# Attention: four steps' weights summed on GpSimd before each group of denominators, and the router's weight product moved into earlier stages

## The reference

```python
x = x + _L0_gnn_ref(_layernorm(x, axis=-1), adj, ...)
x = x + _L0_ffn_ref(_layernorm(x, axis=-1)[None], ...)[0]

# in the second layer
scores = jnp.einsum('bhqd,bhkd->bhqk', q, k) / jnp.sqrt(jnp.float32(HD))
scores = jnp.where(causal, scores, -jnp.inf)
attn = jax.nn.softmax(scores, axis=-1)
y = jnp.einsum('bhqk,bhkd->bhqd', attn, v)
return y.transpose(0, 2, 1, 3).reshape(b, s, d) @ w_o
...
logits = xf.astype(jnp.float32) @ w_router.astype(jnp.float32)
```

## Time and profile before

| | |
|---|---|
| median of three executions | 2271.41 us (2270.23 to 2273.5) |
| the profiled execution | 2268.96 us |
| its span, first to last instruction | 2267.2 us |
| busy in it: PE, DVE, ACT, POOL | 2055.1, 1553.6, 1078.9, 584.4 us |
| mean granted TensorE clock | 0.952 |
| first values product of the attention to its last | 1009.0 to 1683.1 us |

### The profile page before, as it was taken

One profiled execution on the slowest core, in us unless ns is written; L12 is line 12 of the kernel. 1 busy time (PEld: TensorE's weight loads), 2 busy tenths in 40 slices (PEclk: granted clock), 3 DMA queues, 4 the chain that ended last, 5 costly groups with the idle time before them and its releaser, 6 DMA issues. The chain is left out here.

```text
span 2267.2 us, 42225 instructions
## 1 busy us (share of the span) xinstructions
PE 2055.1 (91%) x17716; PEld 1213.2 (54%) x17716; DVE 1553.6 (69%) x2563; ACT 1078.9 (48%) x1059; POOL 584.4 (26%) x447
## 2 busy tenths in 40 slices
PE   6899999999996899989999999999991599999997
PEld 3554444444442344544444444444430599999997
DVE  6679999999984666757777778768347544444442
ACT  4868988989890333213444444444430233323331
POOL 2610000000002012333454555555340222222211
PEclk8989999999998999969999999999995699999999
DMA  6521212212115013343103121010203444444431
GB/s 227 182 79 51 72 52 74 69 52 78 49 52 199 25 47 102 130 112 72 36 16 87 31 64 49 20 38 10 80 24 130 158 121 121 121 121 121 116 66 24
DMA packets 90905, 185.87 MB, mean 82 GB/s; under 512 B 14332, under 2 KB 23548, under 8 KB 86332
## 3 DMA queue, kind: packets, MB, share of 16 engines
q1 hardware_dynamic: 81756, 162.20, 21.8%
q0 software_dynamic: 8960, 20.98, 5.0%
HBM read 138.47 MB, written 40.23 MB: 79 GB/s over the span
## 5 line engine op out<-in xcount | busy, mean ns | idle before, releaser
L1473 DVE TENSOR_REDUCE t_rm<-t_m 128x1 f32<-128x512 f32 (+3 forms) x640 | 372.8, 605 | 150.2 <-PE t_m L1622 96.8
L1407 ACT ACTIVATE t_E<-t_s 128x1024 f32<-128x1024 f32 (+3 forms) x320 | 277.4, 895 | 412.3 <-PE t_s L1639 223.8
L1369 POOL TENSOR_TENSOR t_total<-t_E 128x1024 f32<-128x1024 f32 (+2 forms) x151 | 292.4, 1947 | 221.4 <-PE t_d L1666 215.6
L573 ACT ACTIVATE m_step<-m_ub,gat_bias 128x2048 bf16<-128x2048 f32 x128 | 250.0, 1989 | 11.1 <-DMA m_ub<-scratch_uac 5.7
L715 PE MATMUL m_bd<-m_mask,m_S 128*32 128x512 bf16 x3072 | 230.4, 379 | 10.9 <-DVE m_mask L663 10.9
L715 PE MATMUL m_bd<-gat_adjT,m_S 128*32 128x512 bf16 x2496 | 201.4, 379 | 4.8 <-PE m_dn L715 4.8
L715 PE MATMUL m_bd<-m_mask,m_neg 128*32 128x512 bf16 x2496 | 189.0, 379 | 0.0
L1996 POOL DMA_INDIRECT out<-e_ye,e_token x40 | 80.7, 2018 | 339.1 <-DVE e_ye L2099 334.4
L2160 PE MATMUL e_h<-e_xTh,e_w1h 128*128 128x320 f32 x512 | 159.1, 311 | 1.4 <-DVE e_xTl L2080 1.4
L2160 PE MATMUL e_h<-e_xTh,e_w1l 128*128 128x320 f32 x512 | 158.8, 310 | 0.0
L2160 PE MATMUL e_h<-e_xTl,e_w1h 128*128 128x320 f32 x512 | 158.8, 310 | 0.0
(11 more groups left out here) (359 smaller groups left out, 4085.7 us busy)
## 6 DMA issues: line engine op xcount, KB each, us to landing
a_adj<-in_adj SPq DMA_DIRECT2D x16, 1024.0 KB, 4.9
m_ub<-scratch_uac SPq DMA_DIRECT2D x16, 1024.0 KB, 5.0
e_w1r<-in_L_ffn_w SPq DMA_DIRECT2D x8, 2048.0 KB, 8.2
e_w2r<-in_L_ffn_w SPq DMA_DIRECT2D x8, 2048.0 KB, 8.8
tq_Q<-scratch_parts SPq DMA_DIRECT2D x36, 256.0 KB, 4.6
gat_scale<-scratch_uac SPq DMA_DIRECT2D x32, 256.0 KB
scratch_parts<-o_hi SPq DMA_DIRECT2D x32, 256.0 KB, 2.2
scratch_parts<-o_lo SPq DMA_DIRECT2D x32, 256.0 KB, 2.7
```

The lines of the kernel that those rows point to most:

```text
L573: act.activation(step(n), ub[h % 2][:, :].rearrange("p (t q) -> p t q", t=T), ACT.Relu, bias=bias[:, j, h:h + 1], scale=BIG).then_inc(step ...
L1369: pool.tensor_tensor(total[:, two, off:BANK], E[a % 3][:, two, off:BANK], E[(a + 1) % 3][:, two, off:BANK], ALU.add).then_inc(summed[z], 1)
L1407: act.activation(E[n % 3][:, two, off:BANK], ps_s[:, two, off:BANK], ACT.Exp, scale=SCALE).then_inc(exp_done[z], 1)
L1473: dve.tensor_reduce(rm[:, h, t, ch:ch + 1], ps_m[i % 2][:, 0:w], AX, ALU.max).then_inc(entry_read, 1)
```

## The change

Two parts. In the attention, `total` now holds the sum over four steps: GpSimd adds in three of four steps (E + E, then total + E twice, `add_step`), and one group of denominators, always 512 columns wide, follows for the four. It stands in TensorE's order in step 4k+5, ahead of `values(4k+5)`, where the group of steps 4k to 4k+3 is taken; there are 40 groups. GpSimd waits for `den_done` of the group before only at the first of its three additions. `BY_VECTOR` covers the same part of the last quad, from step 144, in the new grouping; rows are added to the residual one step later in GpSimd's order. In the first stages, the clearing of WG and the scaling of G move to `stage_sequence` (the latter ahead of the product of tile 14), columns 0 and 1 of WG follow the last transposes of that stage, column 2 stands ahead of the first transposes of `stage_factors`, column 3 between its second and third; ScalarE copies the first two at the end of `stage_sequence` and the others where it copied all four.

```diff
+WG_EARLY = 2
+def router_columns(pe, keep, bank, k):
+    for b in range(KD):
+        mm = pe.matmul(bank[:, EXPERTS * k:EXPERTS * (k + 1)], keep["woT"][:, b, k * P:(k + 1) * P],
+                       keep["G"][:, b, :], start=(b == 0), stop=(b == KD - 1))
+    return mm
 # stage_sequence, GpSimd
+                pool.memset(keep["WG"][:, :, :], 0.0).then_inc(g_ready, 1)
                 for t in range(T - 1):
+                    if t == T - 2:
+                        pool.wait_ge(late_in, 16 * (KD + 2))
+                        pool.tensor_tensor(keep["G"][:, :, :], keep["G"][:, :, :], ..., ALU.mult).then_inc(g_ready, 1)
 # stage_sequence, ScalarE, behind store(T - 1)
+                act.wait_ge(wg_early, WG_EARLY)
+                act.activation(keep["WG"][:, 0:WG_EARLY, 0:EXPERTS], ...)
 # stage_sequence, TensorE, behind turn(T - 1)
+                pe.wait_ge(g_ready, 2)
+                for k in range(WG_EARLY):
+                    router_columns(pe, keep, ps_t[0], k).then_inc(wg_early, 1)
 # stage_factors, TensorE
                     if n == 0:
+                        router_columns(pe, keep, late, WG_EARLY).then_inc(wg_full, 1)
                         pe.wait_ge(u_ready, 1)
                     if n == 2:
+                        for k in range(WG_EARLY + 1, KD):
+                            router_columns(pe, keep, late, k).then_inc(wg_full, 1)
                         pe.wait_ge(exp_done, 1)
...
-                pe.wait_ge(g_ready, KD + 3)
-                for k in range(KD):
-                    for b in range(KD):
-                        mm = pe.matmul(p1[...], woT[:, b, k * P:(k + 1) * P], G[:, b, :], ...)
-                mm.then_inc(wg_full, 1)
 # stage_attention
+    FOUR = 4
+    SUMS = []
+    for n in range(QUADS * NS):
+        first_pair = 2 if STEPS[n % NS - n % FOUR + 1][2] else 1
+        SUMS.append((SUMS[-1] if n else 0) + (first_pair, 0, 1, 1)[n % FOUR])
-    BY_VECTOR = [k for k in range(QUADS * NS // 2) if 2 * k >= (QUADS - 1) * NS + HALF + 1]
+    BY_VECTOR = range((QUADS - 1) * NS + HALF + FOUR, QUADS * NS)
+        def add_step(eng, n, z):
+            off, two = STEPS[n % NS][2], slice(2 * z, 2 * z + 2)
+            eng.wait_ge(exp_done[z], n + 1)
+            if n % FOUR == 1:
+                if n >= FOUR:
+                    eng.wait_ge(den_done, n // FOUR)
+                if off:
+                    eng.tensor_copy(total[:, two, 0:off], E[(n - 1) % 3][:, two, 0:off]).then_inc(summed[z], 1)
+                before = E[(n - 1) % 3]
+            else:
+                eng.wait_ge(summed[z], SUMS[n - 1])
+                before = total
+            eng.tensor_tensor(total[:, two, off:BANK], before[:, two, off:BANK],
+                              E[n % 3][:, two, off:BANK], ALU.add).then_inc(summed[z], 1)
 # GpSimd
-                for k in range(QUADS * NS // 2):
...
+                for n in range(QUADS * NS):
+                    if n % FOUR:
+                        for z in range(1 if n in BY_VECTOR else 2):
+                            add_step(pool, n, z)
+                    if n >= (QUADS - 1) * NS:
+                        while added < EARLY and STEP_OF[added] < n % NS - 2:
                             add_row(added)
 # ScalarE
-                            act.wait_ge(summed[z], SUMS[(n - 3) // 2 + 1])
+                            act.wait_ge(summed[z], SUMS[n - 3])
 # VectorE
-                        if s % 2 and (q * NS + s) // 2 in BY_VECTOR:
-                            pair_sum((q * NS + s) // 2)
+                        if s % FOUR and q * NS + s in BY_VECTOR:
+                            add_step(dve, q * NS + s, 1)
 # TensorE
                     for h in range(G):
-                        mm = pe.matmul(ps_d[h * DH:(h + 1) * DH, off:BANK], ones[:, :], total[:, h, off:BANK],
-                                       start=(kt == 0), stop=last)
+                        mm = pe.matmul(ps_d[h * DH:(h + 1) * DH, :], ones[:, :], total[:, h, :],
+                                       start=(kt == 0), stop=(kt == 4 * c))
-                        if n >= 2 and n % 2 == 0:
-                            denominators(n // 2 - 1)
+                        if n > FOUR and n % FOUR == 1:
+                            denominators(n // FOUR - 1)
...
-                denominators(QUADS * NS // 2 - 1)
+                denominators(QUADS * NS // FOUR - 1)
```

More of the change, by code:

```diff
@@ L191, in _ @@
                 store(T - 1)
+                act.wait_ge(wg_early, WG_EARLY)
+                act.activation(keep["WG"][:, 0:WG_EARLY, 0:EXPERTS],
+                               ps_t[0][:, 0:WG_EARLY * EXPERTS].rearrange("p (k e) -> p k e", k=WG_EARLY), ACT.Copy)
             @block.vector
@@ L304, in stage_factors @@
         p2 = st.ps("p2", [P, BANK])
+        late = st.ps("late", [P, BANK])
         link, pm_ready, pmT, dg_ready, M_full = (sem("f_" + n) for n in ("link", "pm", "pmT", "dg", "M"))
@@ L309, in stage_factors @@
         keep["u_out"], keep["ac_out"] = rows_out, rest_out
-        G, WG, woT, parts8 = (keep[n] for n in ("G", "WG", "woT", "parts8"))
-        late_in, g_ready, wg_full = sem("a_late_in"), sem("f_g"), sem("f_wg")
+        WG, parts8 = keep["WG"], keep["parts8"]
+        p_ready, wg_full = sem("f_p8"), sem("f_wg")
         with nc.Block() as block:
@@ L365, in _ @@
                 act.activation(uac[:, 1:3, :, :], uac[:, 1:3, :, :], ACT.Exp).then_inc(exp_done, 1)
-                act.wait_ge(wg_full, 1)
-                act.activation(WG[:, :, 0:EXPERTS], p1[:, TILE:2 * TILE].rearrange("p (k e) -> p k e", k=KD), ACT.Copy)
+                act.wait_ge(wg_full, KD - WG_EARLY)
+                act.activation(WG[:, WG_EARLY:KD, 0:EXPERTS],
+                               late[:, WG_EARLY * EXPERTS:KD * EXPERTS].rearrange("p (k e) -> p k e", k=KD - WG_EARLY), ACT.Copy)
             @block.tensor
@@ L1358, in _ @@
                 added = 0
-                for k in range(QUADS * NS // 2):
-                    a = 2 * k
-                    wide, off = STEPS[a % NS][2], STEPS[(a + 1) % NS][2]
-                    if k >= 1:
-                        pool.wait_ge(den_done, k)
-                    for z in range(1 if k in BY_VECTOR else 2):
-                        pool.wait_ge(exp_done[z], a + 2)
-                        two = slice(2 * z, 2 * z + 2)
-                        if wide < off:
-                            pool.tensor_copy(total[:, two, wide:off], E[a % 3][:, two, wide:off]).then_inc(summed[z], 1)
-                        pool.tensor_tensor(total[:, two, off:BANK], E[a % 3][:, two, off:BANK],
-                                           E[(a + 1) % 3][:, two, off:BANK], ALU.add).then_inc(summed[z], 1)
-                    if a >= (QUADS - 1) * NS:
-                        while added < EARLY and STEP_OF[added] < a % NS - 1:
+                for n in range(QUADS * NS):
[4 more added lines that the diff above has]
+                        while added < EARLY and STEP_OF[added] < n % NS - 2:
                             add_row(added)
@@ L1657, in denominators @@
                 def denominators(k):
-                    q, s = divmod(2 * k, NS)
+                    q, s = divmod(FOUR * k, NS)
                     c, kt, off = STEPS[s]
-                    last = kt == 4 * c + 2
                     if kt == 0 and k:
```

37 lines of the change are left out of this document (11 added, 26 removed).

## The result

The changed kernel took 2323.98 us (median of five, 2321.23 to 2328.75) against 2271.63: a ratio of 1.0228, 95% interval 1.0212 to 1.0244. It is 52 us slower where 14 us less was forecast. The profiled execution has a span of 2322.3 us.

A forecast was written before the change was run, and what follows sets the result against it. TensorE bounds the attention (busy 151 of 160 us). Diagonal 3.8, last half quad 2.6, long 6.0, middle 2.8 give 15.2; less tail 2.7 and clock 3.4, plus router 4.7: 13.8 saved, median 2257.6 us, range 2246 to 2270.

The forecast's parts named there:

- The router's part: End of stage_factors: moving the router's product into TensorE's gaps starts the next stage earlier, saving 4.7 us, bounds 3 and 6.
- the one on the divisions: Attention: VectorE's multiplications fall into GpSimd's additions, some 2 us more per chunk, mostly hidden by VectorE's idle time.
- The term of the clock: Attention: new TensorE waits bring two more stretches at clock 0.50, costing 3.4 us, bounds 0 and five.
- Rival 3: Attention: multiplications held by GpSimd's additions make TensorE wait, 37 us in all, so slower, 2295 us; chance 0.11.
- The groups saved: Attention, TensorE: fewer groups of denominators save 24 x 0.88 + 15 x 0.45 = 27.9 us without anything in the way.
- The floor of GpSimd's chain: Full attention windows: three successive additions on the one tile total allow 15.4 us at least from group to group.
- the short windows: Four attention windows of 15.36 to 15.60 us, held by GpSimd at 15.4, gaining 0.
- the middle ones: Seven attention windows of 15.85 to 15.93 us, gaining 0.4 each, 2.8 us in all.
- The long one: One of ten full attention windows of 16.5 to 21.5 us, gaining 0.6 each, 6.0 us in all.
- the diagonal one: Attention windows of diagonal steps, far above GpSimd's 9.7 us chain: 15 gain 0.25 each, 3.8 us in all.
- the waits for ScalarE and its buffer: Attention: ScalarE refills step 4k's buffer only after GpSimd's first addition, so TensorE stands 0.5 us; 0.2 taken for diagonal groups.
- The tail: End of the attention: GpSimd's last sums end later and the last group is 0.44 longer, costing 2.7 us.

The follow-up runs named there:

- The run with reciprocals: Kernel before, GpSimd untouched, with six extra 48-column reciprocals by VectorE in each of seven chunks, about 2.7 us each time: 2301.92 us, ratio 1.0129.
- nothing held: Changed kernel with the minus sign put on in VectorE's PSUM copy, multiplications on GpSimd (last two chunks stay with VectorE), maxima loads issued earlier: 2259.39 us, ratio 0.9951.
- pairs: Kernel before (denominators every second step) with the router's part and the same edits that leave nothing on VectorE held: 2252.39 us, ratio 0.9919.

## Why the prediction was wrong

**The router's part was right.** Forecast 4.7 (3 to 6), measured 4 (1 to 7.5); the next stage began at 119.20, earlier than the 120.5 to 121 that was to be seen, 1.4 us of it because this execution had come to the last transposes earlier. From there on it gave 5.0, since columns 0 and 1 ran ahead of 107.6, beside work of the others, and delayed nothing.

**The step that failed is the one on the divisions**, with its last sentence, that TensorE feels what exceeds VectorE's idle time, kept "inside the 0.3 of the long windows". The size of the holding was right, in part by luck: some 2 us more per chunk were forecast, (57.1 - 26.9)/14 = 2.2 were measured, but 1.0 of it comes from the first of the four, which was to add nothing. Three things about it were wrong.
- Where it falls. The first of a chunk's four was to find GpSimd waiting, the three others to wait 0.9, 1.6 and 0.6. In fact the first took longest, 2.8 us and through two additions, in six of the fourteen chunks; in the eight others it took 0.28 to 0.40.
- What TensorE feels. VectorE's 5 us of idle time are a sum over a window of 17.6; between VectorE and TensorE stand two banks, so the six delays of 2.8 us in one piece were waits of 2.1 to 2.4, however idle VectorE is later. The run with reciprocals shows this without any holding: 2.7 us in one piece cost 4.2.
- The minus sign, which was not in the working at all: 8.8 us instead of 2.6, and 20.6 where the multiplications were gone. The Trainium skill, SBUF — State Buffer, Who interferes with whom, names instructions with one source that can run in a mode with both ports, tensor_scalar among them, beside those with two SBUF inputs; the prediction drew on that section for the multiplications only. The trace agrees that both kinds are held (2.84 us for a multiplication that takes 0.28, 3.73 for a minus sign that takes 0.17), and that the maxima are not (685 ns before, 683 afterwards); the reciprocals were not held either (943 ns in both kernels). Whether the minus sign ran in such a mode no trace shows. The section gives the ports to the instruction that came first for the whole of it; here the one that waited did not always get its turn when that one ended.

**The term of the clock was mis-sized most**: two more stretches, 3.4 us, bounds nothing to five. There were 31 more of 3.41 us, some 53 us. It was taken as a term by itself, while much of it belongs to the waits: in the changed kernel TensorE had nine waits of 2.1 to 3.4 us for VectorE, and at each the clock fell, from 0.8 us ahead of the wait's end to 0.8 behind it, for one to three stretches, 55 us in all. For the rest of the 141 us (35 at the start, 51 elsewhere) no single wait is shown; but with nothing held only 17 us at 0.50 are left behind the start, so most of it goes with the holding too. Rival 3's mechanism was the one that came, at its place; its chance of 0.11 was the error. Its sizes were not the measured ones: it had 37 us of waits and nothing for the clock, where TensorE's waits for VectorE grew by 17.5 us, 5 in each quad and not the 10 that were to be its sign, and the clock took some 53. By the waits alone its point of decision, 0.25 us felt for each multiplication, was passed by little (17.5/56 = 0.31). The groups saved (27.9) and the waits for VectorE and ScalarE (17.5 + 10.7) about cancel, and the clock is left as the loss.

**The rest of the attention** can be read in the run with nothing held, where the forecast's other steps stand alone. The price of a group held: 0.79 to 0.88 for 0.88, 0.43 for 0.45. The floor of GpSimd's chain held: 15.41 for 15.4, and it shows as forecast for the short windows (nothing gained) and the middle ones (0.5 for 0.4). The long one gained 0.16 instead of 0.6, and the diagonal one lost 0.51 instead of gaining 0.25: there the waits for ScalarE and its buffer, taken as 0.2, took 0.94 (14.08 against 13.14). Not all diagonal windows lost: that from 117 to 121 gained 0.43 (14.16 to 13.73). The sign that the forecast named for the chain, groups released by GpSimd's sums in some ten windows, came: 13 groups start 0.14 to 0.15 us behind the end of a sum, though the profile lists idle time of TensorE for five of these and the tail alone, 4.8 us. The last half quad gained 2.7 from values(145) to values(157), where 2.6 were forecast.

**The tail** was forecast at -2.7, bounds -1.5 and -4. The last group started 5.0 us behind the values of step 157 before, now 8.4 (1726.82 to 1735.20): 3.4, and 0.4 or more for the wider group.

```profile
1735.20 1.08 PE L1682 MATMUL t_d<-t_total,k_ones 128*32 128x512 f32 x4 [3.69 <-POOL t_total L1270]
```

(The view ends within the group.) That is at the bound. With this wait, 3.69 us instead of 1.60, 6.8 us at 0.50 came, which are in no term: the first instruction of the next stage came 47.7 us behind values(157) instead of 41.3, and with nothing held 48.2 instead of 43.6 with pairs.

## What to carry to other kernels

Before work is added to GpSimd, list the instructions of VectorE that it can hold, those with one operand too, and ask of each how long TensorE can go on without it: buffers between the two count there, not VectorE's idle share. A wait of TensorE of some 2 us has a second price, the stretch at the lower clock that comes with it; in the changed kernel the waits grew by 28 us and the lower clock took some 53. And a saving on the engine that bounds is worth nothing where it lengthens the chain between two of its steps: here 3.8 us in five windows were to be had, and with a single `total` and three buffers E 0.1 of them were left.

## What was unexpected of the hardware

- A held instruction of VectorE did not always get in between two queued additions of GpSimd. In the changed kernel, six multiplications that came 0.30 to 0.40 us ahead of an addition's end waited for the next one too (2.8 us), while three that came 0.30, 0.41 and 0.44 ahead got in (0.4 to 0.6 us), and so did those that came earlier (1.1 to 2.3 us). Without multiplications, the minus sign that came 1.4 us ahead of an end also waited for the next addition (3.73 us). What decides stays open.
- Cutting the additions in two did not shorten the longest hold: 2.87 us became 3.43, three short additions in place of two long ones.
- Not every held instruction costs something. In the last half quad VectorE's normalisations of finished rows (128x512, one operand, 0.54 us when free) took up to 2.6 us in the changed kernel and in that with nothing else held, and the latter's windows there gained what was forecast all the same.
- 19.0 us of VectorE's time in seven pieces cost 29 us, although VectorE has idle time in every window, by way of 62 us more at the lower clock.
